# A decoder kernel on one core: another order of work in the merged turns and around the pairs' queries

## The reference, cut to what matters

```python
x = x + encoder(layernorm(x), ...)      # 4 layers: linear attention (16 heads of 8), then relu(h @ W1) @ W2
x = x + cross_attention(layernorm(x), ctx, mask)          # 16 heads, softmax
x = x + bit_linear_ffn(layernorm(x))                      # quantized, depthwise convolution, silu
x = x + topk_attention(layernorm(x))                      # 16 heads, the 64 largest of 128 scores kept
x = x + channel_attention(layernorm(x), ctx)              # 2 sets, 4 heads of 32 channels
x = x + experts(layernorm(x))                             # sum over 8 of (silu(x @ Wg) * (x @ Wu)) @ Wd
```

```python
scores = jnp.einsum('bhqd,bhkd->bhqk', q, k) / np.sqrt(D_HEAD)
_, idx = jax.lax.top_k(scores, TOP_K)
logits = jnp.where(knn_mask, scores, -jnp.inf)            # knn_mask is True at idx
attn = jnp.einsum('bhqk,bhkd->bhqd', jax.nn.softmax(logits, axis=-1), v)
```

## Time and profile before

| | us |
|---|---|
| median of 3 runs | 1395.84 (1394.71 to 1397.26) |
| the profiled execution | 1398.07 |
| its span, first to last instruction | 1396.3 |
| PE busy | 1046.0 (75%) |
| DVE busy | 961.9 (69%) |
| ACT busy | 679.3 (49%) |
| POOL busy | 474.8 (34%) |
| mean granted TensorE clock | 0.828 of full speed |

### The profile page before, as it was taken

The page is one execution under the profiler, slowest core; times in us unless marked ns, Lnnn a source line. Parts: engine busy times, 40 slices in busy tenths (PEclk is TensorE's granted clock), DMA queues, the critical chain, the costliest instruction groups (busy, mean ns, idle before and its releaser), DMA issues.

```text
span 1396.3 us, 17900 instructions
## 1 busy us (share of the span) xinstructions
PE 1046.0 (75%) x5079; PEld 690.8 (49%) x5082; DVE 961.9 (69%) x3098; ACT 679.3 (49%) x1774; POOL 474.8 (34%) x461
## 2 busy tenths in 40 slices
PE   5888846655767278877575689778998865888999
PEld 4766713334445145554443344433444444666887
DVE  7555587987577887778878868545668678665332
ACT  4444437433666245665237634265667634633321
POOL 4333347410654144445237500333334403311100
PEclk9999957766878678887577789999998986989999
DMA  4100110000000000000010001011110120222343
GB/s 138 29 23 30 29 32 1 1 0 1 10 22 10 5 18 14 18 9 1 1 54 1 1 22 61 23 46 50 54 46 23 50 76 23 70 90 77 122 147 116
DMA packets 41762, 53.88 MB, mean 39 GB/s; under 512 B 6448, under 2 KB 20672, under 8 KB 41664
## 3 DMA queue, kind: packets, MB, share of 16 engines
q1 hardware_dynamic: 41488, 52.24, 12.0%
q0 software_dynamic: 176, 0.53, 0.1%
HBM read 51.71 MB, written 1.05 MB: 38 GB/s over the span
## 4 chain that ended last, share of the span: by engine, by line
PE 48%; DVE 28%; ACT 9%; issue 7%; POOL 6%; DVEq 1%; DMA 0%; POOLq 0%; SPq 0%; ACTq 0%
PE psum L1739 7%; PE psum L1750 6%; PE psum L1725 6%; PE psum L1816 2%; PE psum L1508 2%; PE psum L1484 2%; PE psum L1603 2%; PE psum L1327 2%; PE psum L1823 2%; PE psum L1466 2%; ACT far L1034 2%; PE psum L1404 2%; PE psum L1557 2%; POOL Wk L711 2%; DVE nmax L2131 1%
## 5 line engine op out<-in xcount | busy, mean ns | idle before, releaser
L2259 DVE TENSOR_TENSOR big<-psum,qe 128x512 f32<-128x512 f32 x106 | 72.9, 688 | 159.8 <-PE psum L1750 76.9
L1187 ACT ACTIVATE qe<-psum 128x512 f32<-128x512 f32 x106 | 62.3, 595 | 127.3 <-PE psum L1739 127.1
L1725 PE MATMUL psum<-big,wexp 128*128 128x256 f32 (+1 forms) x340 | 117.4, 461 | 0.0
L1034 ACT ACTIVATE far<-far,half_far,fmul 128x128 bf16<-128x128 bf16 x256 | 103.0, 488 | 22.9 <-DVE hit L2034 22.9
L2047 DVE MAX8 near<-Wk 128x8 f32<-128x128 f32 x512 | 103.0, 276 | 0.0
L668 POOL TENSOR_SCALAR veps<-mv 128x4 f32<-128x4 f32 x35 | 8.8, 252 | 267.0 <-DVE mv L1953 267.0
L766 POOL TENSOR_TENSOR Wk<-Wk,far 128x1024 f32<-128x1024 f32 x32 | 68.2, 2135 | 70.3 <-ACT far L1034 70.3
L1725 PEld LDWEIGHTS psum<-big,wexp 128*128 128x128 f32 x340 | 70.5, 207 | 31.0 <-issue 22.3
L1750 PE MATMUL psum<-xin,wexp 128*128 128x512 f32 x128 | 70.0, 630 | 13.7 <-DVE far L2259 8.3
L1404 PE MATMUL psum<-ident,Wk 128*128 128x128 f32 x256 | 48.6, 360 | 42.1 <-POOL Wk L711 39.3
L1739 PE MATMUL psum<-xin,wexp 128*128 128x512 f32 x128 | 77.7, 693 | 2.4 <-DVE vaug L2699 1.5
(11 more groups left out here) (359 smaller groups left out, 2867.5 us busy)
## 6 DMA issues: line engine op xcount, KB each, us to landing
wexp<-in_mg SPq DMA_DIRECT2D x48, 256.0 KB, 2.6
wexp<-in_mu SPq DMA_DIRECT2D x48, 256.0 KB, 3.0
wexp<-in_md SPq DMA_DIRECT2D x48, 256.0 KB, 3.1
w<-in_aw SPq DMA_DIRECT2D x8, 256.0 KB, 2.8
w<-in_w2a SPq DMA_DIRECT2D x8, 256.0 KB, 2.6
wqkv<-in_aw SPq DMA_DIRECT2D x8, 192.0 KB, 2.2
ctxt<-in_ctx SPq DMA_DIRECT2D x5, 256.0 KB, 4.2
xin<-in_x SPq DMA_DIRECT2D x4, 256.0 KB, 2.9
```

Of the source, the lines that this page charges most:

```text
L1034: ins = act.activation(far[t][:, hd, :], far[t][:, hd, :], ACT.Identity, bias=half_far[:, 0:1], scale=fmul[t][:, hd:hd + 1])
L1187: act.activation(sg_of[k >= EARLY][k % 2], bank(5 + k % 2), ACT.Silu).then_inc(silu_done, 1)
L1725: mm = pe.matmul(bank(4)[:, 0:w], wd[l % 2][:, c + j, :], hid_of[k >= EARLY][k % CH][:, j * w:(j + 1) * w], start=first and j == 0, stop=l ...
L2259: dve.tensor_tensor(hid_of[k >= EARLY][k % CH], bank(U_BANK[k]), sg_of[k >= EARLY][k % 2], ALU.mult).then_inc(hu_done, 1)
```

## The change

Four things are reordered; no arithmetic is added or removed.

In the merged turns PE issues the up product's first two chunks directly behind the feed-forward's turned input, the other two ahead of the second half of `turned_scores`, the down product ahead of `outputs(b - 2)`, and `outputs` in two parts behind `scores(b + 1, 0)` and behind the next attention input. ACT does the next step's attention input ahead of all sixteen signs, and the feed-forward's input at the end of the turn before, between queries and keys; `maxima` and the relus change places with penalties. DVE does `step_normalize("A", b + 2)` ahead of `attend(b + 1, "output")`.

In the second half, for a top-k turn in which a pair's channel attention prepares its queries (b = 12 and b = 14), POOL's `signed_scores(b)` goes from point 0 to point 2 and waits until DVE has the queries (`c_q`). For the groups 2 to 5 POOL scales and shifts the keys four to six points earlier (at r = -5 and -4 in place of 0 and 2) and adds the base two points later (6 in place of 4).

```diff
@@ POOL topk
-                if p == 0 and lo <= b < hi:
+                pair = next((g for g in range(2, NG) if CH_START[g] == (b - 1) * PTS + 10), None)
+                if p == (0 if pair is None else 2) and lo <= b < hi:
+                    if pair is not None:
+                        pool.wait_ge(c_q, 4 * pair + 4)
                     signed_scores(b)
@@ POOL channel
-                if r == 0:
+                key_scaled, key_shifted, based = (0, 2, 4) if g <= 1 else (-5, -4, 6)
+                if r == key_scaled:
...
-                if r == 2:
+                if r == key_shifted:
...
-                if r == 4:
+                if r == based:
@@ ACT merged_turn
-                if 0 <= b - 1 < NB:
-                    maxima(b - 1)
-                if fed:
+                if fed and b == STEPS - 1:
                     feed(b, "input")
                 if here:
                     penalties(b, range(0, 6))
+                if fed:
+                    feed(b, 0)
+                if 0 <= b - 1 < NB:
+                    maxima(b - 1)
+                if here:
+                    penalties(b, range(6, 11))
                 if old:
                     exponentials(b - 2, 0)
...
                 if fed:
-                    feed(b, 0)
-                if here:
-                    penalties(b, range(6, 11))
+                    feed(b, 1)
                 if old:
                     exponentials(b - 2, 1)
...
-                if fed:
-                    feed(b, 1)
                 if here:
                     penalties(b, range(11, H))
...
-                    signs(b + 1, range(0, 6))
                 if after:
                     attend(b + 2, "input")
                 if new:
-                    signs(b + 1, range(6, H))
+                    signs(b + 1, range(0, H))
                 if after:
                     attend(b + 2, "queries")
+                    feed(b + 1, "input")
                     attend(b + 2, "keys")
@@ DVE merged_turn
+                if fed or b == -1:
+                    step_normalize("A", b + 2)
                 if step:
                     attend(b + 1, "output")
-                if fed or b == -1:
-                    step_normalize("A", b + 2)
```

More of the change, by code:

```diff
@@ L1637, in merged_turn @@
                     cross_queries(1, 1)
-                if fed:
-                    feed(b, 1)
-                if old:
-                    outputs(b - 2, 0)
-                    outputs(b - 2, 1)
                 if step:
@@ L1646, in merged_turn @@
                     feed(b, "down")
-                if old:
-                    outputs(b - 2, 2)
-                    outputs(b - 2, 3)
                 if step:
@@ L1653, in merged_turn @@
                     scores(b + 1, 0)
+                if old:
+                    outputs(b - 2, 0)
+                    outputs(b - 2, 1)
+                if new:
                     scores(b + 1, 1)
@@ L1656, in merged_turn @@
                     attend(b + 2, "input")
+                if old:
+                    outputs(b - 2, 2)
+                    outputs(b - 2, 3)
+                if after:
                     attend(b + 2, "projections")
```

## The result

| | time, us | ratio to before |
|---|---|---|
| before | 1395.74 median (1394.71 to 1397.26) | |
| changed | 1385.48 median (1384.26 to 1386.59, 4 runs) | 0.9926, 95% interval 0.9913 to 0.9939 |
| predicted | 1359 (1348 to 1385) | |

The change wins 10.3 us where 37 were forecast. The profiled execution took 1385.35 us (span 1383.6) against 1398.07.

The account below looks back on a forecast made before the run. No engine was full; DVE's waits in the merged turns (56.7 us) were the target, with DVE the bound afterwards. Merged turns 30 plus pairs 7 gave 37 us off, so a median of 1359 us, range 1348 to 1385.

Parts of the forecast that it names:

- Down product: Merged turns: it ends 3.7 us earlier, DVE waits 1.25 us and not 4.5; 17.5 us won over the turns.
- The attention product's wait: Merged turns: DVE's 6.4 us in six turns go except 2.4 in turn 0; 4 us won.
- Output, scores, projections: Merged turns: PE begins projections at about 594.1, DVE's wait of 2.4 us goes, DVE bounds the turn; 15 us won.
- PE's clock: Merged turns: outputs ahead of projections may keep the clock up and halve projections; counted 0, since DVE is the bound.
- Norm A's wait for the root: Merged turns: norm A now waits for POOL's root, with 0.3 us slack; up to 1.5 us wait in turn 0.
- The sum of the merged turns: Merged turns: waits won 36.5 us, less 6.5 for costs, gives 30 us; a turn takes 31.3 against 37.57.
- the moves: Merged turns: cost of norm A's root and later ACT keys, 0.8 us a turn, 6.5 us in eight turns.
- The pairs' turns: Turns 12 and 14: POOL's collision with DVE's normalizations removed; 7 us won, including 1.4 for a warmer PE; upper bound 11.5.
- PE wins its waits, 2.19 + 4.45: Turns 12 and 14: PE's waits for the pair's queries go, 6.6 us won.
- The collision of queries with signed scores: Merged turns, second rival: later keys let POOL go first, 3.4 us lost in each of seven turns; 1383 us, chance 0.10.
- The third, half the gain: Merged turns: ACT takes over, turns of 34.5 us, about 18 won, 23 with pairs; 1373 us, chance 0.19.
- The fourth, slower: Merged turns: norm A ahead of the residual holds DVE for a late root; 1400 us at 4 us late; chance 0.09.

Follow-up runs that it names:

- e12: e4's kernel with six of eight products left out of each second half of the first step's outputs, so heads are missing; 1372.8 us, one run.
- e8: Changed kernel with the last four penalties of turns 12 and 14 behind the experts' first gate on ScalarE; 1367.6 us, ratio 0.9799.
- e4: Changed kernel with VectorE's order residual, head outputs, norm F, dropped marks; 1383.9 us, ratio 0.9922.
- e2: Kernel before with the change to the merged turns alone, GpSimd's code the old one; 1383.6 us, ratio 0.9909.
- e7: Changed kernel with three extra 128 x 512 products on TensorE where it waits in turn 9, result overwritten; 1377.5 us, ratio 0.9856.
- e10: e2's kernel with the last four penalties of turns 12 and 14 behind the experts' first gate; 1379.1 us, ratio 0.9889.
- e9: Changed kernel repeated as it is; 1381.8 us, ratio 0.9908, runs from 1378.0 to 1387.0.
- e1: Kernel before with the change to GpSimd's code alone, the merged turns the old ones; 1395.5 us, ratio 0.9996.
- e11: Changed kernel with both the edit of e5 and that of e8; 1366.0 us, ratio 0.9798.
- e5: Changed kernel with the second half of the first step's outputs ahead of the next input's transposes on TensorE; 1375.3 us, ratio 0.9855.
- e6: e5's kernel with VectorE's order residual, head outputs, norm F, dropped marks besides; 1380.5 us, ratio 0.9891.

## Why the prediction was wrong, step by step

**Down product.** Right. Its wait in a steady turn was to go from 4.5 to 1.25 us and is 1.69 in turn 5; the last relu ended at 564.9, ahead of the product's start at 566.2, as I had it. The attention product's wait, 6.4 us in six turns, was to go but for 2.4 in turn 0, and one of 2.0 us is left, in turn 0.

**Output, scores, projections.** This step failed, in one clause: "the outputs now lie in the time in which PE waited for ACT". The projections were to begin 28.4 us into the turn and began at 31.0 (580.54 less 549.52). Of these 2.6 us 2.2 are the outputs in front of them, which ran at the low clock: sixteen in 3.4 us, against the 1.69 that I read from the earlier trace rows at the high one and took along to another place. Even at that they would have ended at 578.96, 0.6 us behind the turned input (578.38), for which I had no term; the other 1.6 are the clock's. I had counted "PE's clock" as 0 since VectorE would be the bound. e12 shows TensorE as the bound, and the two turns of e8 agree, with 1.9 us between them at 0.91 and 0.85 of the clock.

**Norm A's wait for the root.** I looked at norm A, where 0.8 us a turn was taken for it and for the later keys together, and it waited 0.37 in turn 5. The wait came at norm F, 1.25 us, which I had not looked at: an operation with two SBUF inputs was moved next to its statistics. e4 shows that it cost nothing in the changed kernel, as TensorE was later still; in e12, where TensorE is not, 1.1 us of waiting at norm F are most of what parts its 32.3 us from my 31.3.

**The sum of the merged turns.** 30 forecast; 16.7 in the first trace, 19.9 to 20.7 in the others with that order (e2, e7 to e10). Turn 5 alone has 3.6 us more than the 31.3 forecast: 0.5 of VectorE's busy time, 0.4 at the down product, 0.4 at norm A, 1.25 at norm F and 1.04 at the projections. Of the missing 10 to 13 us e12 gives back 6 to 7.5 (26.4 against 19.9 and, in e4, 18.9): for these TensorE's last third is shown as the cause. The rest is in part turn 3, the one with the long way. It took 61.4 us before, 62.6 in the changed kernel's first trace, 61.4 in e9 and 60.6 in e12. Its wait at the down product was 2.8 us and is 2.9, and its wait for the projections went from 2.5 to 1.04, while 1.6 us for the root came; by the terms of my sum (2.8 less 1.25 and 2.5 less 0.3, less the 0.8 for the moves) it was to win some 3 us. What then remains stays open.

**The pairs' turns.** The collision was read rightly and its removal happened, normalization 0.58 us. The step "PE wins its waits, 2.19 + 4.45" failed. I took the wait for what it ended with and did not ask what TensorE would wait for next. ScalarE's gate, in turn 12 1.1 us behind the end of that wait (1075.78 in the trace of before), was fixed by its own queue; in turn 14 it stood 1.6 us ahead of it (1176.96 against 1178.59). In the changed kernel, where the queries come early, it stands 3.3 us behind their product in both turns (1063.14 against 1059.81, 1165.15 against 1161.83). In the earlier trace rows there is no row of ScalarE; I never asked for one. The two chains are of like length, so that shortening one was worth 0 (e1: 0.3 us over both turns) and both 7.6 and 8.1 (e8, e11), near my 7 and under the 11.5 that I gave as upper bound. That it is near is no merit of the sum: its 1.4 us for a warmer PE came from no row, and the first four groups of products behind the gate of turn 12 take 4.2 us in e8 where they took 7.6 in the changed kernel.

**The rest.** 8.5 us were lost in turn 9 and the cross stage and 4.5 won ahead of 355 us, where no instruction was moved. In turn 9 it is the clock's level at the same instructions; from 240 to 350 us the mean granted clock is 0.71 against 0.67 before. I had no term for that; the spread of the kernel's own times (e9, 9 us) is of that size, and the 2.8 us that I gave as what can be told from no change was too little. The range ended 0.5 us short, and that it came so near is luck: its upper end, 1385, was put there for a collision that did not come.

**The rivals.** The collision of queries with signed scores did not come: in turn 5 the queries end 0.1 us ahead of it, as before (and in turn 3 they take 4.10 us, as before). The third, half the gain, had the right size for the merged stage (18 us), but named ScalarE; it was TensorE there, as far as is shown, and ScalarE in the pairs. The fourth, slower, did not come.

## What to carry to other kernels

When a wait goes, look up on every engine what else the waiting instruction's successors need, and whether that has moved at all; if a second chain is as long, cut both or neither. A duration of TensorE is only valid at the granted clock of its place, so a moved product is priced at both levels, and a gain that only shows in the total of one run is first checked by stage against the same code elsewhere. Between a statistic and the root that another engine makes of it, let no operation stand that locks that engine out, though here something else was later still.

## What had not been expected of the hardware

- The granted clock fell from 1.00 to 0.50 in a stretch in which TensorE had been without idle time for 8 us (e5, 572.5), and stayed at 1.00 across waits of 1.0 us elsewhere (e4, turn 9).
- A wait of 1.5 us less was worth 3 us, since the products behind it took 1.1 us each and not 2.1 (e8, turn 12).
- Runs of one kernel on one chip differ by up to 16 us (e6, 1375.0 to 1391.1), and part of that arises in stretches with the same code, 4 to 5 us ahead of 355 us and 5.9 in turn 9.
- A table load cost ScalarE 1.30 us from end to next start, with no drain behind it.
